# A fused cross-attention and FFN kernel: another order of loads, norms and copies in the first stage, and another split of the last FFN unit's work among the engines

## What is computed

```python
# layer 0, cross-attention, residual on x
Q = layernorm(x) @ Wq.T + bq;  K = ctx @ Wk.T + bk
x = x + softmax(Q @ K.T / sqrt(512)) @ ctx
# layer 0, dense FFN with a routed low-rank part, residual
# layer 1, cross-attention: 32 query heads, 8 key/value heads of 128, RMS norms on q and k, residual
# layer 1, FFN with int4-like weights in groups of 128, residual
h = layernorm(x)
x = x + (silu(h @ gate) * (h @ up)) @ down        # H = 512, I = 1792 = 14 units of 128
```

## Time and profile before

| | |
|---|---|
| time, median of 3 runs | 858.44 us (857.34 to 859.26) |
| the profiled execution | 859.67 us, its span 858.0 us |
| mean granted TensorE clock | 0.993 of full speed |
| PE busy, PEld busy | 822.0 us (96%), 673.7 us (79%) |
| DVE, ACT, POOL busy | 565.8 (66%), 536.5 (63%), 553.5 us (65%) |
| DMA | 131.34 MB, mean 153 GB/s |

### The profile page before, as it was taken

The page is one execution under the profiler, slowest core; times in us unless marked ns, Lnnn a source line. Parts: engine busy times, 40 slices in busy tenths (PEclk is TensorE's granted clock), DMA queues, the critical chain, the costliest instruction groups (busy, mean ns, idle before and its releaser), DMA issues.

```text
span 858.0 us, 13297 instructions
## 1 busy us (share of the span) xinstructions
PE 822.0 (96%) x3920; PEld 673.7 (79%) x3920; DVE 565.8 (66%) x990; ACT 536.5 (63%) x1769; POOL 553.5 (65%) x557
## 2 busy tenths in 40 slices
PE   6899999999899999999999999999997899999995
PEld 4687888788788888888888888888885677777773
DVE  5606752533566666666666666666666789999996
ACT  4543561144777777777776777776675467777763
POOL 3332562321577777777777777777776258999995
PEclk9999999999999999999999999999999999999999
DMA  7511567203566666666667766667654123343302
GB/s 269 179 50 29 143 164 203 66 1 111 165 205 194 186 185 186 185 186 186 187 188 223 224 192 188 180 194 227 187 159 120 52 74 147 147 148 148 141 7 99
DMA packets 99350, 131.34 MB, mean 153 GB/s; under 512 B 25998, under 2 KB 71950, under 8 KB 99279
## 3 DMA queue, kind: packets, MB, share of 16 engines
q1 hardware_dynamic: 99278, 130.49, 50.3%
HBM read 90.61 MB, written 39.85 MB: 152 GB/s over the span
## 4 chain that ended last, share of the span: by engine, by line
PE 83%; DVE 6%; DMA 4%; ACT 2%; POOL 2%; issue 1%; SPq 1%; POOLq 0%; DVEq 0%; ACTq 0%
PE pair L1433 19%; PE pair L1435 19%; PE pair L1434 19%; PE pair L1591 8%; PE pair L1592 8%; PE pair L1685 6%; DMA land<-block_bounce 2%; DMA block_bounce<-tb 1%; PE pair L1453 1%; DVE kv L1302 1%; DMA resid<-in_x_dram 1%; PE pair L1492 1%; PE pair L1543 1%; PE pair L1548 1%; PE pair L1520 1%
## 5 line engine op out<-in xcount | busy, mean ns | idle before, releaser
L1433 PE MATMUL pair<-split,xnT_hi 128*128 128x512 f32 x288 | 113.3, 394 | 0.3 <-issue 0.3
L1435 PE MATMUL pair<-split,xnT_lo 128*128 128x512 f32 x288 | 112.1, 389 | 0.0
L1434 PE MATMUL pair<-split,xnT_hi 128*128 128x512 f32 x288 | 112.1, 389 | 0.0
L909 ACT ACTIVATE headT<-land,wqk 128x512 f32<-128x512 f32 x64 | 46.3, 724 | 89.8 <-DMA land<-block_bounce 60.8
L1433 PE MATMUL pair<-split,aoT_hi 128*128 128x512 f32 x256 | 101.3, 396 | 0.0
L934 ACT ACTIVATE prob<-pair,nmax 128x128 f32<-128x128 f32 x256 | 90.3, 364 | 17.3 <-DVE nmax L1269 16.5
L1435 PE MATMUL pair<-split,aoT_lo 128*128 128x512 f32 x256 | 100.9, 394 | 0.0
L1434 PE MATMUL pair<-split,aoT_hi 128*128 128x512 f32 x256 | 100.5, 393 | 0.0
L704 POOL TENSOR_TENSOR prob<-prob,rinv 128x512 f32<-128x512 f32 x64 | 66.7, 1043 | 43.9 <-DVE rinv L1239 43.9
L1591 PE MATMUL pair<-xnT_hi,split 128*128 128x512 f32 x224 | 91.3, 408 | 3.3 <-ACT kv L1000 1.3
L1592 PE MATMUL pair<-xnT_lo,split 128*128 128x512 f32 x224 | 88.5, 395 | 0.0
(11 more groups left out here) (152 smaller groups left out, 2135.5 us busy)
## 6 DMA issues: line engine op xcount, KB each, us to landing
block_bounce<-tb SPq DMA_DIRECT2D x244, 128.0 KB, 2.3
land<-block_bounce SPq DMA_DIRECT2D x61, 512.0 KB, 3.2
raw<-in_wqo_dram SPq DMA_DIRECT2D x62, 256.0 KB, 2.9
kv<-in_ffn_w_dram SPq DMA_DIRECT2D x14, 768.0 KB, 4.4
kv<-in_ffn_z_dram SPq DMA_DIRECT2D x14, 768.0 KB, 5.7
kv<-key_bounce SPq DMA_DIRECT2D x32, 128.0 KB, 2.7
key_bounce<-tb SPq DMA_DIRECT2D x44, 64.0 KB, 2.0
resid<-in_x_dram SPq DMA_DIRECT2D x2, 1024.0 KB, 9.6
```

Source lines behind the costliest of these rows:

```text
L1433: pe.matmul(dst, l_hi, r_hi, start=first, stop=False)
L1434: pe.matmul(dst, l_hi, r_lo, start=False, stop=False)
L1435: return pe.matmul(dst, l_lo, r_hi, start=False, stop=last)
```

## The change

It has two parts.

*First stage.* SP issues all twelve chunks ahead of x; the small loads come between x's halves. DVE makes all eight low parts of the context ahead of its work on x; then statistics 0 to 3, 4, 5, norms 0 to 3, statistics 6 and 7, norm 4, low parts 0 to 3, norms 5 to 7, low parts 4 to 7. The norms use four buffers and the first four transposes four banks. POOL makes the low parts of all four Wk chunks, then the first rstd, two Wq chunks, the second rstd, the rest. PE issues ten products of `ident` with itself into bank 7 ahead of everything; transposes tiles 0 to 3 behind item 6 (once ACT has copied six items), 4 and 5 behind item 8, 6 and 7 behind item 9. The q items go by token half: 8 to 11 need tiles 0 to 3 only, 12 to 15 the others. ACT's order follows.

*Last FFN unit.* The product with silu(gate) stays in its PSUM bank (no `tb`), and ACT and DVE split it from there. ACT takes position 9 (D0) and now also D1 (into tmp_c) ahead of last_hi(0); POOL gets the add of tmp_c (1024 columns, `s_p1`) ahead of that of tmp_b, and gives up (1,0). DVE gives up D1 and gets (1,0): six halves. The down products run in the order 0, 1, 2, 3 in other banks (`LAST_SLOT`), of which block 2's is that of the product itself.

```diff
@@ -227,10 +227,18 @@
+            if k == 0:
+                return (headT[:], score, prob[:], sq)[t % HALF]
             return kv[:, 2 * QUART + t * D:2 * QUART + (t + 1) * D] if k == 3 else (headT, score)[t % 2][:]
+        def kq_item(n):
+
+            return (n // 2, n % 2) if n < 2 * KT else (n % KT, (n - 2 * KT) // KT)
+
         def ln_bank(k, t):
+            if k == 0:
+                return bank[(4, 5, 6, 7, 4, 5, 4, 5)[t]]
             return bank[(4, 5, 0, 1, 4, 5, 7, 0)[t] if k == 3 else t % 4 if k == 1 else 4 + t % 2]
@@ -351,6 +359,7 @@
         s_pb = sem("down_added_from_b")
+        s_p1 = sem("last_down_one_added")
         s_oc = sem("out_copied")
@@ -442,10 +451,14 @@
-        LAST_DOWN = (0, 3, 1, 2)
+        LAST_DOWN = (0, 1, 2, 3)
+        LAST_SLOT = (11, 13, 10, 12)
         def last_bank(c, h):
-            return 2 * pair_of(LAST, None, ITEMS + 2 + LAST_DOWN.index(c)) + h
+            return 2 * pair_of(LAST, None, LAST_SLOT[c]) + h
+
+        def last_sum_bank(h):
+            return bank[2 * pair_of(LAST, None, SIDE) + h][:]
@@ -465,12 +478,13 @@
                     load(3 * k + 1 + h, ctxT[k, :, h * D:(h + 1) * D])
-                if k in (1, 2):
-                    half = slice(HALF * (k - 1), HALF * k)
-                    sp.dma_start(resid[:, half, :], x[half].rearrange("b p d -> p b d")).then_inc(s_x[k - 1], 16)
-            for dst, src in ((bias, bqk), (nw, norm_w), (mask_sb, mask), (gb, gate_b.to_broadcast([P, NR])),
-                             (gds, ffn_s)):
-                sp.dma_start(dst[:], src).then_inc(s_small, 16)
+            for h in range(2):
+                tiles = slice(HALF * h, HALF * (h + 1))
+                sp.dma_start(resid[:, tiles, :], x[tiles].rearrange("b p d -> p b d")).then_inc(s_x[h], 16)
+                if h == 0:
+                    for dst, src in ((bias, bqk), (nw, norm_w), (mask_sb, mask), (gb, gate_b.to_broadcast([P, NR])),
+                                     (gds, ffn_s)):
+                        sp.dma_start(dst[:], src).then_inc(s_small, 16)
@@ -625,13 +639,13 @@
-            for k in range(2):
+            for k in range(KT):
                 lo(3 * k)
             ln_rstd(0, 0)
-            lo(3 * 2)
-            lo(3 * 3)
+            for c in range(WQ0, WQ0 + 2):
+                lo(c)
             ln_rstd(0, 1)
-            for c in range(WQ0, WFFN):
+            for c in range(WQ0 + 2, WFFN):
                 lo(c)
@@ -755,14 +769,16 @@
                 tmp, done = (tmp_a, s_pa) if c == 0 else (tmp_c, s_pb)
-                pool.wait_ge(s_ta, by_scalar(LAST, 9) + 2 + e)
+                pool.wait_ge(s_ta, by_scalar(LAST, 9) + 3 + e)
                 pool.wait_ge(done, LAST - 1)
...
             pool.wait_ge(s_ta, by_scalar(LAST, 9) + 1)
+            pool.tensor_tensor(accT[:, 1, :], accT[:, 1, :], tmp_c, ALU.add).then_inc(s_p1, 1)
+            pool.wait_ge(s_ta, by_scalar(LAST, 9) + 2)
             pool.tensor_tensor(accT[:, 3, :], accT[:, 3, :], tmp_b, ALU.add).then_inc(s_pb, 1)
-            for e, (h, c) in enumerate(((0, 0), (0, 3), (1, 0))):
+            for e, (h, c) in enumerate(((0, 0), (0, 3))):
                 last_added(e, h, c)
@@ -789,22 +805,19 @@
                 hi(c)
-            for t in range(2):
-                ln_hi(0, t)
-            hi(WQ0)
...
             for n in range(4 * KT):
-                m, h = (n % (2 * KT)) // 2, n % 2
+                m, h = kq_item(n)
                 is_q = n // (2 * KT)
...
                                bias=bias[:, KT * (1 - is_q) + m:KT * (1 - is_q) + m + 1]).then_inc(s_kqe, 1)
-                if n + 2 < T:
-                    ln_hi(0, n + 2)
-                if 1 <= n < KT:
-                    hi(WQ0 + n)
+                if 2 <= n < 2 + KT:
+                    hi(WQ0 + n - 2)
+                for t in {6: range(HALF), 8: (4, 5), 9: (6, 7)}.get(n, ()):
+                    ln_hi(0, t)
                 if 2 * KT <= n < 3 * KT:
@@ -1059,19 +1072,22 @@
                 act.wait_ge(s_hm, UNITS + 1 + h)
-                act.activation(unit_h(LAST % 2, 0)[:, half(h)], hidden[:, half(h)], ACT.Copy).then_inc(s_hh, 1)
-
+                act.activation(unit_h(LAST % 2, 0)[:, half(h)], last_sum_bank(h), ACT.Copy).then_inc(s_hh, 1)
+
+            take(LAST, None, 9, tmp_a, down_s[:, 1 - LAST % 2, 0:1])
+            take(LAST, None, SUM, tmp_c, down_s[:, 1 - LAST % 2, 1:2])
             last_hi(0)
-            take(LAST, None, 9, tmp_a, down_s[:, 1 - LAST % 2, 0:1])
             last_hi(1)
...
             act.wait_ge(s_ds, UNITS)
-            for e, (h, c) in enumerate(((0, 0), (0, 3), (1, 0))):
+            for e, (h, c) in enumerate(((0, 0), (0, 3))):
                 act.wait_ge(s_it, item(LAST, 13) + KT * h + LAST_DOWN.index(c) + 1)
...
                     act.wait_ge(s_pa, LAST - 1)
+                else:
+                    act.wait_ge(s_p1, 1)
                 act.activation((tmp_a if c == 0 else tmp_c)[:, half(h)], bank[last_bank(c, h)][:], ACT.Copy,
@@ -1099,7 +1115,9 @@
                 dve.wait_ge(s_rstd, 2 * k + group + 1)
-                if n >= 2 and k != 3:
+                if k == 0 and t >= HALF:
+                    dve.wait_ge(s_xt, n - HALF + 1)
+                elif k in (1, 2):
                     dve.wait_ge(s_xt, n - 1)
@@ -1118,18 +1136,23 @@
                     ctx_lo(3 * k + 1 + h)
-                if k in (1, 2):
-                    if k == 2:
-                        ln_norm(0, 0)
-                        ln_norm(0, 1)
-                    dve.wait_ge(s_x[k - 1], 16)
-                    ln_stats(0, k - 1)
+            dve.wait_ge(s_x[0], 16)
+            ln_stats(0, 0)
+            dve.wait_ge(s_x[1], 16)
+            ln_tile_stats(HALF)
+            ln_tile_stats(HALF + 1)
+            for t in range(HALF):
+                ln_norm(0, t)
+            ln_stats(0, 1, done=2)
             dve.wait_ge(s_small, 80)
             dve.tensor_tensor(wqk[:], nw[:, 0:1], nw[:, 1:2], ALU.mult).then_inc(s_wqk, 1)
-            for t in range(T):
+            ln_norm(0, HALF)
+            for t in range(HALF):
                 ln_lo(0, t)
-                if t + 2 < T:
-                    ln_norm(0, t + 2)
+            for t in range(HALF + 1, T):
+                ln_norm(0, t)
+            for t in range(HALF, T):
+                ln_lo(0, t)
@@ -1387,7 +1410,7 @@
             def last_sum(h):
-                cur = bank[2 * pair_of(LAST, None, SIDE) + h][:]
+                cur = last_sum_bank(h)
                 if h == 0:
@@ -1395,25 +1418,28 @@
                 dve.wait_ge(s_si, UNITS + 1)
-                times_silu(LAST, half(h), cur, None)
+                dve.tensor_tensor(cur, cur, gated(LAST % 2)[:, half(h)], ALU.mult).then_inc(s_hm, 1)
...
                 dve.wait_ge(s_hh, UNITS + h)
-                dve.tensor_tensor(unit_h(LAST % 2, 1)[:, half(h)], hidden[:, half(h)],
+                dve.tensor_tensor(unit_h(LAST % 2, 1)[:, half(h)], last_sum_bank(h),
                                   as32(unit_h(LAST % 2, 0)[:, half(h)]), ALU.subtract).then_inc(s_hl, 1)
...
             last_lo(0)
-            take_down(LAST, None, SUM, 1, False)
             last_lo(1)
...
             dve.wait_ge(s_ds, UNITS)
-            for h, c in ((0, 1), (0, 2), (1, 3), (1, 1), (1, 2)):
+            for h, c in ((0, 1), (0, 2), (1, 0), (1, 1), (1, 2), (1, 3)):
                 dve.wait_ge(s_it, item(LAST, 13) + KT * h + LAST_DOWN.index(c) + 1)
-                dve.wait_ge(s_tv, by_vector(LAST, SIDE) + 1)
+                dve.wait_ge(s_tv, by_vector(LAST, 8) + 1)
+                if c == 0:
+                    dve.wait_ge(s_pa, LAST - 1)
+                if c == 1:
+                    dve.wait_ge(s_p1, 1)
                 if c == 3:
@@ -1444,6 +1470,8 @@
                     pe.wait_ge(s_xlo, n - 3)
+                elif k == 0 and t < HALF:
+                    pe.wait_ge(s_kqe, 6)
                 elif k == 1:
@@ -1455,8 +1483,11 @@
             pe.wait_ge(s_const, 5)
+            for _ in range(10):
+                pe.matmul(bank[7][:, tile(0)], ident[:], ident[:], start=True, stop=True)
+
             def kq0(n, k):
-                m, h = (n % (2 * KT)) // 2, n % 2
+                m, h = kq_item(n)
                 is_q = n // (2 * KT)
@@ -1473,21 +1504,21 @@
                     kq0(n, k)
-                    if k == KT - 2 and n in (3, 5):
-                        ln_transpose(0, n // 4)
-                    if k == KT - 1:
-                        ln_transpose(0, n + 2)
             for n in range(6, 4 * KT):
...
                     lo_done(pe, WKEY - 1)
+                    pe.wait_ge(s_xlo, HALF)
+                if n == 3 * KT:
                     pe.wait_ge(s_xlo, T)
...
                     kq0(n, k)
+                for t in {6: range(HALF), 8: (4, 5), 9: (6, 7)}.get(n, ()):
+                    ln_transpose(0, t)
...
                 if b % HALF == 0:
-                    pe.wait_ge(s_kqe, 4 * KT - 1 + b // HALF)
```

(15 more changed lines are left out.)

## The result

| | before | changed |
|---|---|---|
| median | 858.10 us (857.34 to 859.26, 4 runs) | 850.46 us (849.96 to 851.62, 4 runs) |
| ratio, 95% interval | | 0.9906 (0.9893 to 0.992) |
| profiled execution, span | 859.67, 858.0 us | 851.62, 850.0 us |
| first score product starts | 61.26 | 53.72 |
| VectorE's last sum starts | 837.04 | 830.40 |

The kernel became 0.9% faster: 7.6 us in the medians, 8.0 in the two profiled spans. I had forecast 853.8 with a range of 850.0 to 856.3. The last three rows split the 8.0. The first stage gave 7.54 (61.26 - 53.72). The long middle took 0.90 back (from 775.78 to 776.68, from the first of these starts to the second). The last unit gave 1.33 (11.16 to 9.83). From the transposes to the end both take 9.8.

The account below looks back on a forecast made before the run. TensorE bounds the kernel with 83% of the chain, busy 763.8 of 780 us, so only its ends can gain: first stage 3.4 plus tail 1.2 makes 4.6 us off 858.44, giving 853.8, range 850.0 to 856.3.

Parts of the forecast that it names:

- the stop at the heart of the sum: First stage: TensorE stands 2.9 us, from 30.0 to 32.9, ahead of item 8, waiting for low parts of x.
- The direction, and the two places: Whole kernel: faster, chance 0.89; only time before 60 us and after 840 us matters, passed on microsecond for microsecond.
- my ledger of the first stage: First stage, 6.20 to 61.42: 55.2 us, of which 6.0 standing and 1.9 slow start are all there is to win.
- The chunk loop: First stage: chunks load ahead of x, chunk 6 at 10.0; TensorE stays fed and the loop ends at 22.7, not 34.18.
- The norms: First stage: rstd pairs of 2.27 and norms slowed beside GpSimd delay low parts of x; item 8 starts at 32.9.
- the same neighbours: First stage: 32.9 chosen for item 8 because the slow, colliding profile rows have the same engines working beside them.
- The bound that I named: First stage: without any of three VectorE meetings with GpSimd, low parts end at 29.9 and TensorE doesn't wait.
- The clock: First stage: a TensorE stop of 2.9 us is followed by half-speed matmuls costing 1.5 us.
- The warm-ups I called hidden by the stop: First stage: if the ten warm-ups don't raise the clock, the loop ends 1.9 us later, hidden by waiting for norms.
- The tail: Last FFN unit: GpSimd's adds start at 837.0, sum to 9.8 to 10.1, and transposes start 1.2 us earlier.
- no stop: Rival: item 8 starts at 30.0, first stage gains 7.8, 849.4 us in all; chance 0.2 including the milder version at 851.
- the 0.43 us steps: Sign: after TensorE's wait ahead of the q items, matmuls run 0.43 us apart.

Follow-up runs that it names:

- The run with norms made late: Changed kernel plus four unused VectorE statistics instructions (2.4 us) ahead of norms 0 to 3; first score product at 59.53 against 53.72 us, item 8 at 33.1.
- Made on purpose, a stop of 2.27: Changed kernel plus four unused VectorE statistics instructions (2.4 us) ahead of low part 0; first score product at 57.57 against 53.72 us.
- the run with the old loads: Changed kernel with SP's loads issued in the order of before, x inside the chunk loop; first score product at 58.51 against 53.72 us.
- the version with the adds shared anew: Changed kernel with VectorE adding all of the first half, ACT with GpSimd adding (1,0) and (1,3); 849.08 and 850.07 us, ratios to before 0.9883 and 0.9895.
- that run: The changed kernel unaltered, executed again; 851.23 us, ratio to before 0.991; its rival said 776 to 777 us again, a middle made longer by the change.
- the run with low parts ahead of norm 4: Changed kernel with four extra statistics instructions ahead of norms 0 to 3, and norm 4 moved behind low parts 0 to 3; first score product at 55.39 us.

## Why the prediction was right, and where it was off

The time, 850.46, lies 0.5 us inside the lower end of my range of 850.0 to 856.3, and not by the way that I forecast: the stop at the heart of the sum didn't take place, and the first stage gave 7.54 where I had 3.4. With both stages' gains and a middle as before (7.54 + 1.33 off 858.44) it would have been 849.6, outside the range. That the number fell inside is luck in part.

**The direction, and the two places.** Right. Everything ahead of the score products is handed through the middle, and the gain is in the 6.0 us of standing and 1.9 of slow start that my ledger of the first stage held: 7.54 of 7.9.

**The chunk loop.** Right. The chunks came somewhat earlier than my 10.0 for chunk 6 (GpSimd begins its low part at 9.72), and the loop ran from 6.31 without a gap to item 6's end at 25.4.

**The norms.** This is the step that failed: "So item 8 starts at 32.9, after 2.9 us of standing". It started at 30.02. Terms were taken from rows with a neighbour that the new order doesn't have. The rstd pair (2.27 in the earlier trace rows) had an add of 1.16 that lay beside two VectorE subtractions, of two SBUF tiles each; alone it takes 0.20, which is 0.96 less, twice. The norms (1.48 in the earlier trace rows) had GpSimd beside them; here they were done 0.45 us before it began, 2.2 less. And x came 0.6 earlier. That is 4.7, of which 1.9 came back: the second rstd stood 1.5 behind GpSimd's chunks 12 and 13, a queue that I passed over (as I did norm 4's wait for tile 0's transposes, which held it as long), and norm 0 stood 0.4 behind the statistics of tiles 4 and 5. 32.9 - 2.8 is 30.1. The bound that I named, 29.9 without any meeting, was the true end; I had weighed the rows by "the same neighbours" where I should have laid the two engines' times side by side. With the rstd pair at 2.27 the norms run from 21.0, and the low part of chunk 12 from 21.9 (its users at 21.3 and ScalarE's 0.6), so they meet. With the pair at 1.3 the norms run from 20.1 to 22.1 and are all but over. The pair, sized with a neighbour, was the term that made the meetings. The run with norms made late shows the other branch: meetings of 1.12 and 1.52. The price of one was about right (1.48), the two meetings of norms 0 to 3 didn't take place.

**The clock.** The 1.5 us fell away with the stop. Made on purpose, a stop of 2.27 cost 1.6. But one of 3.42 in the run with the old loads cost nothing, so "a stop of 2.9 us is on the dear side" isn't a rule. The changed kernel never put it to the test. The warm-ups I called hidden by the stop were worth 2.8 against the execution without them.

**The tail.** 1.33 against 1.2, and by the way described: ScalarE's take first, GpSimd's five adds back to back, 9.57 us from 830.52 to 840.09 where I had 9.8 to 10.1, no add of 2.73 among them. That GpSimd sets the start of the output transposes is shown for the changed kernel by the version with the adds shared anew: it moved only who adds what, and with that what the transposes wait for, and gained 1.4. For the kernel before it rests on the times alone, 848.03 and 848.20.

**The sum.** 3.4 + 1.2 forecast, 7.54 + 1.33 measured, less 0.9 in the middle, which I had at nothing. The middle was 775.78 before and 776.68 and 776.20 in two executions of the changed kernel, which is what the rival of that run had said; but it was 774.74 and 777.67 in two executions of one other kernel, and 773.7 to 775.6 in the eight others. Two things in the traces account for most of this scatter. TensorE stood for 13.5 to 16.6 us between 62 and 825. And the granted clock fell to half in up to three places between 60 and 830, which cost 0 to 5.2 us (the part of full speed that was missing, times the length, in windows of 5 us). In the kernel with the adds shared anew these were 13.9 and 3.4 in the first execution, 16.1 and 5.2 in the second; the run without warm-ups, with the shortest middle, had no such place. With both taken off, all thirteen middles lie between 756.2 and 757.8. For the change that leaves 1.3 more standing and 1.7 less of low clock, and a rest that is 1.3 longer, within the scatter of the rests. Whether any of the 0.9 comes with the change stays open, and so does why the gains of the two parts' medians add to 6.9 and not 8.9.

The likeliest rival by the result was my "no stop" (849.4 with the tail, given a fifth together with half a stop): 850.46 and the lost 0.9 fit it. Its condition was the one that came true: GpSimd's chunks came when the norms were over. Of the signs that I had named for my own case, the loop's end near 22.7 and GpSimd's adds back to back came; the stop, the 0.43 us steps and a first score product near 58 didn't.

## What to carry to other kernels

A duration with a neighbour is two numbers, one alone and one met; before using either, put both engines' new timelines side by side and see whether they meet. Where two cases differ by an order of arrival and the bounds lie 3 us apart, that order is the prediction. And the engine whose adds are last isn't always the one the chain names: count which of its results the wait asks for, then let the other engine do the half that is needed first.

## What the runs showed of the hardware

**The shared port.** Norms from SBUF to SBUF on VectorE took 0.53 to 0.54 alone and 0.93 to 1.60 with a GpSimd subtraction beside them; GpSimd's own small add took 0.20 alone and 1.16 beside VectorE's subtractions of two SBUF tiles. Low parts that read PSUM kept 0.6 apart in either case. The dearer meetings were those with more of GpSimd's instruction left: in the run with late norms the norm that started 0.46 us behind it took 1.12, the one 0.25 behind the next took 1.52. GpSimd paid as well, 1.48 for that second subtraction where 1.29 is usual. The Trainium skill's page SBUF — State Buffer, section Who interferes with whom, has both directions, and that the order of issue decides who is blocked. Norm 4 of the changed kernel, 0.2 us behind its neighbour, took 1.33 and agrees; in the run with low parts ahead of norm 4 a norm started at 22.16, 0.02 ahead of GpSimd's subtraction, and was the one held (1.60), so starts this close don't tell who is blocked. The 1.3 that my prediction gave for each meeting by a full block is more than any of them cost: 0.4 to 1.1.

**The slow start.** TensorE's pace changed 4.0 us after the first matmul in before (9 slow ones) and 5.7 us after it in the changed kernel without warm-ups (13). The profile's granted clock reads 1.00 over both stretches (5 to 12 us), so the slow start is read from the spacing alone, 0.43 against 0.23. The Trainium skill's page TensorE: Matmul & The Clock Gate, section What's actually happening, says that this moment varies between runs, since what watches the activity isn't started by the kernel; the two executions, of two kernels, do differ, by 1.7 us. The ten warm-ups (fp32, 128 columns, 4.0 to 4.6 us in all) beforehand were enough in all ten profiles of kernels that have them: their first chunk product starts at full speed.

**Stops.** Behind stops of TensorE of 1.57 (31.68, low parts ahead of norm 4), 1.79 and 2.08 (both in the last unit of before), 1.89 and 3.42 us matmuls went on at full pace, with a granted clock of 1.00. Behind 2.25, 2.27, 2.61 and 2.87 us they did not, for some seven to twelve matmuls 0.43 apart, and the granted clock of those stretches was 0.59 to 0.93 in windows of 5 us (0.66 from 235 to 240 us in before), a mean over time at 1.2 and at 2.4 GHz. In before with the warm-ups a shorter stop, 1.76 us ahead of 840.12, was followed by a fall to 0.50. The length of the stop alone didn't decide it.
